# Attention with rope and a gated FFN: high parts of the rope rows on ScalarE, low parts first on GpSimd, swaps ahead of a transpose, span 0 held twice

## The reference

```python
q_pe = _rope(q_pe, cos, sin)            # the 64 rope rows of every query
k_pe = _rope(k_pe[:, None, :, :], cos, sin)
qs = concat([q_nope, q_pe]); ks_ = concat([k_nope, k_pe])
scores = einsum('bhqd,bhkd->bhqk', qs, ks_) * scale
scores = where(causal, scores, finfo.min)
attn = softmax(scores)
out = einsum('bhqk,bhkd->bhqd', attn, v) @ wo
```

## Time and profile before

| what | value |
|---|---|
| runs before | 1123.23 us median of 3 (1123.19 to 1127.71) |
| profiled execution | 1121.26 us, its span 1119.5 us |
| mean granted TensorE clock | 0.949 |
| busy share | PE 88%, PEld 75%, DVE 69%, ACT 67%, POOL 70% |

### The profile page before, as it was taken

The page is one execution under the profiler, slowest core; times in us unless marked ns, Lnnn a source line. Parts: engine busy times, 40 slices in busy tenths (PEclk is TensorE's granted clock), DMA queues, the critical chain, the costliest instruction groups (busy, mean ns, idle before and its releaser), DMA issues.

```text
span 1119.5 us, 26361 instructions
## 1 busy us (share of the span) xinstructions
PE 980.7 (88%) x10560; PEld 837.8 (75%) x10560; DVE 775.7 (69%) x1095; ACT 750.6 (67%) x1093; POOL 783.0 (70%) x576
## 2 busy tenths in 40 slices
PE   5558998989898989898989899988989896879998
PEld 5547777878687868786878777777878785768887
DVE  5747777877776778777787777867777787653134
ACT  1328687878686868777778777777778785752232
POOL 3656969596959796978688858877797877822331
PEclk7869999999998999999999989999999999889999
DMA  5019999999999999999989998899999999992001
GB/s 165 9 48 178 159 176 171 191 159 180 173 170 165 180 171 183 171 168 169 181 165 180 164 173 165 168 161 179 176 167 179 173 169 192 181 171 76 1 19 58
DMA packets 591979, 170.24 MB, mean 152 GB/s; under 512 B 574064, under 2 KB 585968, under 8 KB 591856
## 3 DMA queue, kind: packets, MB, share of 16 engines
q1 hardware_dynamic: 587376, 167.89, 83.1%
q10 hardware_dynamic: 4480, 0.66, 0.4%
HBM read 15.41 MB, written 2.10 MB: 16 GB/s over the span
## 4 chain that ended last, share of the span: by engine, by line
POOL 40%; PE 20%; DMA 9%; issue 8%; SPq 8%; ACT 7%; DVE 6%; ACTq 1%; POOLq 0%
POOL hl L1105 18%; PE s_ps L528 9%; POOL pe L1105 6%; PE s_ps L626 5%; DMA pT<-hl 5%; POOL QB_lo L1105 4%; POOL q_swap L1105 4%; DMA q_swap<-q_pe 3%; ACT hl L731 3%; SPq L471 3%; SPq L457 3%; POOL QA_lo L1105 3%; ACT prob L804 3%; POOL QA_hi L1105 3%; DVE hl L952 2%
## 5 line engine op out<-in xcount | busy, mean ns | idle before, releaser
L1105 POOL TENSOR_TENSOR hl<-prob,hl 128x1024 f16<-128x1024 f32 (+4 forms) x256 | 386.1, 1508 | 111.3 <-ACT hl L731 95.6
L804 ACT ACTIVATE prob<-s_ps,neg_max 128x1024 f32<-128x1024 f32 (+7 forms) x384 | 318.2, 863 | 184.8 <-POOL hl L1105 132.8
L943 DVE TENSOR_REDUCE part_max<-s_ps 128x1 f32<-128x1024 f32 (+7 forms) x256 | 245.4, 988 | 182.5 <-PE s_ps L626 165.8
L731 ACT ACTIVATE hl<-prob 128x1024 f16<-128x1024 f32 (+7 forms) x384 | 296.5, 806 | 25.3 <-DMA pT<-hl 23.4
L642 PE MATMUL o_ps<-v,pT 128*128 128x65 f16 x2176 | 232.3, 195 | 14.6 <-DMA pT<-hl 12.2
L643 PE MATMUL o_ps<-v,pT 128*128 128x64 f16 x2176 | 232.6, 197 | 0.0
L644 PE MATMUL o_ps<-v,pT 128*128 128x65 f16 x2176 | 231.3, 193 | 0.0
L952 DVE TENSOR_TENSOR hl<-prob,hl 128x1024 f16<-128x1024 f32 (+3 forms) x128 | 203.8, 1592 | 38.3 <-ACT hl L731 37.1
L642 PEld LDWEIGHTS o_ps<-v,pT 128*128 128x128 f16 x2176 | 206.5, 98 | 16.5 <-DMA pT<-hl 13.9
L644 PEld LDWEIGHTS o_ps<-v,pT 128*128 128x128 f16 x2176 | 205.8, 100 | 0.0
L643 PEld LDWEIGHTS o_ps<-v,pT 128*128 128x128 f16 x2176 | 205.2, 98 | 0.0
(11 more groups left out here) (183 smaller groups left out, 1992.1 us busy)
## 6 DMA issues: line engine op xcount, KB each, us to landing
q_swap<-q_pe SPq DMA_DIRECT2D x128, 64.0 KB, 2.0
pT<-hl SPq DMA_TRANSPOSE x256, 4.7
wq_sb<-in_L_attn_wq_dram SPq DMA_DIRECT2D x8, 384.0 KB, 4.1
acc<-in_L_attn_x_dram SPq DMA_DIRECT2D x4, 512.0 KB, 6.5
wo_sb<-in_L_attn_wo_dram SPq DMA_DIRECT2D x8, 256.0 KB, 3.2
x_in<-in_L_attn_x_dram SPq DMA_DIRECT2D x1, 2048.0 KB, 8.3
out_dram<-y SPq DMA_DIRECT2D x8, 256.0 KB, 2.1
wkvs<-in_L_attn_wkv_b_dram SPq DMA_DIRECT2D x8, 128.0 KB, 4.0
```

What stands on the lines that cost most here:

```text
L731: return nc.scalar.activation(dst, src, ACT.Copy)
L804: nc.scalar.activation(prob_of(u, m), score_bank(u, m), ACT.Exp, bias=neg_max[:, r:r + 1]).then_inc(exp_done, 1)
L943: nc.vector.tensor_reduce(part_max[:, u % 2, m:m + 1], src, AX.X, ALU.max).then_inc(part_done, 1)
L1105: return lambda: nc.gpsimd.tensor_tensor(dst, a, b, op)
```

## The change

- ScalarE's `rope_of_b` becomes `rope_high`: after `rope.2` it makes the high part of head A, the copy `pe_b`, and the high part of head B, three copies instead of one, and waits for the former group's `B..lo`. It stands in units 3, 5, 11 and 13 (before, the single copy stood in 4, 6, 12 and 14). GpSimd's eight high parts a pair fall away. `pe_b` is held once.
- GpSimd's order in a unit is `low`, `rest`, steps. A group has its three rope steps in one unit (2, 4, 10, 12) and both low parts in the next (3, 5, 11, 13). `wkvs`, `wpe_hi` and `wpe_lo` stay in their units.
- SP issues the swaps of a unit ahead of its `turn_first`.
- `prob0` is held twice; the exponential of span 0 of unit u waits for `low` of unit u-2.
- In the setup, the low parts of head B are made around `rope(0)`, and VectorE no longer makes the high part of head A.

```diff
-POOL_NEXT = {1: ["wkvs"], 6: ["wpe_hi"], 7: ["wpe_lo"], 10: rope(3)[:1], 11: rope(3)[1:] + ["A3hi"], 12: ["A3lo", rope(0)[0], "B3hi"],
...
+POOL_NEXT = {1: ["wkvs"], 6: ["wpe_hi"], 7: ["wpe_lo"], 10: rope(3), 11: ["A3lo", "B3lo"], 12: rope(0), 13: ["A0lo", "B0lo"]}
...
-        prob0 = ab("prob0", [P, W0])
+        prob0 = ab("prob0", [P, 2, W0])
...
             for u in range(NU):
                 pair, k = divmod(u, PU)
-                turn_first(u)
                 for name in jobs_at(u - 1):
                     if name[0].startswith("qB"):
                         swap(int(name[0][2:]), name[1])
+                turn_first(u)
                 turn_rest(u)
...
-            def rope_of_b(g, pair):
+            def rope_high(g, pair):
 
                 n = group_no(g, pair)
                 act.wait_ge(pool_done, POOL.after((f"rope{g}.2", pair)))
-                if n >= 2:
-                    before = GROUP_ORDER[(n - 2) % NG], (n - 2) // NG
+                if n >= 1:
+                    before = GROUP_ORDER[(n - 1) % NG], (n - 1) // NG
                     act.wait_ge(pool_done, POOL.after((f"B{before[0]}lo", before[1])))
-                copy(pe_b[:, n % 2, :], pe[ROPE:P, n % 2, :]).then_inc(rope_b, 1)
+                if pair > 0:
+                    act.wait_ge(scores_ready, queries_free(1, g, pair))
+                copy(queries(Q_hi, 0, g)[0:ROPE, :], pe[0:ROPE, n % 2, :])
+                copy(pe_b[:], pe[ROPE:P, n % 2, :])
+                copy(queries(Q_hi, 1, g)[0:ROPE, :], pe[ROPE:P, n % 2, :]).then_inc(rope_hi, 1)
 
             def exponentials(u, m):
                 act.wait_ge(max_ready, 2 * u + 1 + m // 2)
-                if m == 0 and u >= 1:
-                    act.wait_ge(pool_done, POOL.after(("low", u - 1)))
+                if m == 0 and u >= 2:
+                    act.wait_ge(pool_done, POOL.after(("low", u - 2)))
...
             for u in range(NU):
                 prob_low(u, 0)
+                prob_low(u, smaller(u))
                 for name in steps_at(u):
                     step(name)
-                prob_low(u, smaller(u))
```

More of the change, by code:

```diff
@@ L178, in rope @@
     return [f"rope{g}.{i}" for i in range(3)]
-def side(h, g):
-    return [f"{h}{g}hi", f"{h}{g}lo"]
 POOL_KEY = [[f"rms{n}"] + [f"kr{n}.{i}" for i in range(6)] for n in range(NG)]
@@ L188 @@
     f"rstd{n}" for n in range(NG)] + [(w, 0) for w in POOL_W] + POOL_KEY[0] + POOL_KEY[1] + [(r, 0) for r in rope(3)] + POOL_KEY[2] + POOL_KEY[3] + [
-    (r, 0) for r in rope(0)] + [(r, 0) for r in side("B", 3) + side("B", 0)]
-POOL_NEXT = {1: ["wkvs"], 6: ["wpe_hi"], 7: ["wpe_lo"], 10: rope(3)[:1], 11: rope(3)[1:] + ["A3hi"], 12: ["A3lo", rope(0)[0], "B3hi"],
-             13: ["B3lo"] + rope(0)[1:], 14: side("A", 0), 15: side("B", 0)}
-POOL_OWN = {2: rope(2)[:1], 3: rope(2)[1:] + ["A2hi"], 4: ["A2lo", rope(1)[0], "B2hi"], 5: ["B2lo"] + rope(1)[1:], 6: side("A", 1),
-            7: side("B", 1)}
+    (r, 0) for r in ["B3lo"] + rope(0) + ["B0lo"]]
+POOL_NEXT = {1: ["wkvs"], 6: ["wpe_hi"], 7: ["wpe_lo"], 10: rope(3), 11: ["A3lo", "B3lo"], 12: rope(0), 13: ["A0lo", "B0lo"]}
+POOL_OWN = {2: rope(2), 3: ["A2lo", "B2lo"], 4: rope(1), 5: ["A1lo", "B1lo"]}
 POOL_FFN = {6: ["up_zero", "up_scale_zero", "down_zero"], 8: ["up_scaled0", "up_scaled1"], 9: ["down_scaled"]}
-ROPE_B_OWN, ROPE_B_NEXT = {4: 2, 6: 1}, {12: 3, 14: 0}
+ROPE_HI_OWN, ROPE_HI_NEXT = {3: 2, 5: 1}, {11: 3, 13: 0}
 def steps_at(u):
@@ L207, in steps_at @@
     return steps
-POOL = Steps(POOL_SETUP + [name for u in range(NU) for name in [("low", u)] + steps_at(u) + [("rest", u)]])
+POOL = Steps(POOL_SETUP + [name for u in range(NU) for name in [("low", u), ("rest", u)] + steps_at(u)])
 def query_cols(g):
@@ L255, in mla_gated_ffn_kernel @@
         pe = ab("pe", [P, 2, BANK])
-        pe_b = ab("pe_b", [LORA, 2, BANK])
+        pe_b = ab("pe_b", [LORA, BANK])
         wq_sb = ab("wq_sb", [P, KE, QW])
@@ L361, in mla_gated_ffn_kernel @@
         queries_split = sem("queries_split")
-        swapped, rope_b = sem("swapped"), sem("rope_b")
+        swapped, rope_hi = sem("swapped"), sem("rope_hi")
         scores_ready, part_done, max_ready = sem("scores_ready"), sem("part_done"), sem("max_ready")
@@ L394, in prob_of @@
             w1 = width(u, 1)
-            return (prob0[:], prob12[:, u % 2, 0:w1], prob12[:, u % 2, w1:W12])[m]
+            return (prob0[:, u % 2, :], prob12[:, u % 2, 0:w1], prob12[:, u % 2, w1:W12])[m]
         def halves_of(u, m):
@@ L828, in _ @@
                 if name == ("qA0", 0):
-                    rope_of_b(3, 0)
-            rope_of_b(0, 0)
+                    rope_high(3, 0)
+            rope_high(0, 0)
             for u in range(NU + 1):
@@ L840, in _ @@
                     pair, k = divmod(u, PU)
[L841 to L844, removed]
+                    if k in ROPE_HI_OWN:
+                        rope_high(ROPE_HI_OWN[k], pair)
+                    if k in ROPE_HI_NEXT and pair < PAIRS - 1:
+                        rope_high(ROPE_HI_NEXT[k], pair + 1)
                     prob_high(u, 1)
@@ L1014, in split_first @@
                 hi, lo = queries(Q_hi, 0, g)[0:ROPE, :], queries(Q_lo, 0, g)[0:ROPE, :]
-                dve.wait_ge(pool_done, POOL.after((f"rope{g}.2", 0)))
-                then_wait(nc.vector.tensor_copy(hi, src))
+                dve.wait_ge(rope_hi, group_no(g, 0) + 1)
                 nc.vector.tensor_tensor(lo, src, f32(hi), ALU.subtract).then_inc(queries_split, 1)
@@ L1137, in split_step @@
                 n = group_no(g, pair)
-                src = (pe_b if head else pe)[0:ROPE, n % 2, :]
+                src = pe_b[:] if head else pe[0:ROPE, n % 2, :]
                 hi, lo = queries(Q_hi, head, g)[0:ROPE, :], queries(Q_lo, head, g)[0:ROPE, :]
[L1140 to L1145, removed]
+                run((name, pair), tt(lo, src, hi.bitcast(F32), ALU.subtract), (rope_hi, n + 1))
             def ffn_step(name):
                 if name == "up_zero":
-                    run(name, memset(up_raw[:, :, IT - 1, :], 0.0), (rope_b, NG * PAIRS))
+                    run(name, memset(up_raw[:, :, IT - 1, :], 0.0), (rope_hi, NG * PAIRS))
                 elif name == "up_scale_zero":
@@ L1228, in _ @@
             rotate_key(3)
+            split_step("B3lo", 0)
             for name in rope(0):
                 rope_step(name, 0)
-            for g in GROUP_ORDER[:2]:
-                for name in side("B", g):
-                    split_step(name, 0)
+            split_step("B0lo", 0)
             for u in range(NU):
                 prob_low(u, 0)
+                prob_low(u, smaller(u))
                 for name in steps_at(u):
                     step(name)
-                prob_low(u, smaller(u))
             for j in range(NG * IT):
```

## The result

| | median of runs | range | profiled execution | its span | mean granted clock |
|---|---|---|---|---|---|
| before | 1123.23 us (5 runs) | 1121.45 to 1127.71 | 1121.26 us | 1119.5 us | 0.949 |
| changed | 1112.44 us (5 runs) | 1110.08 to 1115.57 | 1112.44 us | 1110.6 us | 0.943 |

The ratio is 0.9917, with a 95% interval of 0.9893 to 0.994: faster by 0.8% by this ratio, and by 10.8 us (1.0%) on the two medians of the table. 1109 had been predicted.

A forecast was written before the change was run, and what follows sets the result against it. TensorE and GpSimd were taken to bound units by turns, some 17 us a pair lost to waits. 7.5 pairs at 2.1 us, less 1.4, gave 14.4 us: 1109 us, own range 1097 to 1117, 8 in 10 1080 to 1137.

The forecast's parts named there:

- The added wait: ScalarE waiting for `rope.2` before its copies: 3.7, 2.3, 2.2 and 3.0 us a pair, 60 to 110 us over the run.
- the slower rival: ScalarE's wait for `rope.2` dominates because the swap lands later: 1132 us, chance 0.23.
- The busy times: Expected engine totals: GpSimd busy near 705 us, ScalarE's copies 38 us more, GpSimd's swap wait still near 50 us.
- The second copy of span 0: ScalarE's exponential no longer waits for `low` of the unit before; unit 3 of pair 3 starts 1.4 us earlier.
- the first rival: The waits eat the whole gain, or the second copy doesn't help: 1117 to 1129, say 1122 us, chance 0.12.
- The gain per pair: Working over pair 3 gave 3.1 us won, less 0.8 for the clock leaves 2.3; 2.1 taken, for 7.5 pairs.
- one such stretch more in a pair: One more slow-clock stretch of TensorE behind unit 3's longer wait, half on the chain: 0.8 us a pair lost.
- the third rival: Every wait throttles TensorE, four slow stretches a pair instead of two: 1127 us; chance 0.07 no change, 0.05 slower.
- The start: In the setup, the first scores wait for three copies of 1.8 us instead of VectorE's 0.42: +1.4 us once.
- `turn_first` behind the swap: On SP, that transpose comes up to 3.0 us later in four units a pair, its product needed later: costed nothing.
- A sign: Listed as showing the forecast wrong: the pair's time changing in units 6 to 9, where no rope step stands.

## Why the prediction was right, and where its steps were not

**The added wait: right.** In pair 3 it was 3.33, 2.28, 3.01 and 2.59 us, where 3.7, 2.3, 2.2 and 3.0 stood in the working; 84.6 us in all, where 60 to 110 were expected. The sine step began 18.0 us after unit 1 (18.45 worked out), the copies ended so that unit 4 was 3.6 us late (4.1 worked out). In pair 3 SP's `turn_rest` of unit 1 took 2.73 us instead of 3.23, and the swap was not late, so the slower rival did not come.

**The busy times: right.** GpSimd 711 us (705), ScalarE +37 (38), the swap's wait 48 (50).

**The second copy of span 0, "1.4 us won": the step that failed.** Unit 3 did start 1.5 us earlier, but both runs that add or remove the copy (ratio 0.9982 on the kernel before, 1110.25 against 1112.44 us on the changed one) show no gain. The half of the first rival that "`hl` and `pT` stay two deep" is what happens on the kernel before, where `hl` waited 76.6 us. In the changed kernel it is another reason: the sum sets unit 4 (23.70 us after unit 1 without the copy, 23.76 with it), and its time doesn't hang on the start of unit 3.

**The gain per pair: mis-sized.** Over 7 pairs, from unit 1 of the first to unit 1 of the last, the changed kernel took 8.8 us less, 1.3 a pair instead of 2.1; the last pair and what follows took 4.0 less where about 1 was expected. In pair 3 the forecast held up to unit 9 (56.43 against 57.05 us from unit 1); then units 9 to 16 were to take 55.3 us and took 58.2, against 57.3 before. I had carried ScalarE's short units 12 and 14 on to the end of the pair; they came (5.9 and 4.5 us), but unit 15 then took 8.0 us instead of 6.6, with an exponential in it that waited 1.34 us for maxima. (The one behind it waited 1.63 us, as it had before.) That TensorE, held up in units 11 and 13, had its work still to do there is my reading and was not tested.

**That the total came so close is partly luck.** 14.4 us had been forecast; 10.8 came on the medians and 8.9 on the profiled executions, which can be taken apart. The seven pairs gave 5.9 us less than forecast and the rest of the kernel 2.9 more, and the start came 3.9 us later, where 1.4 had been worked out, for a reason that isn't the change's (below).

**The clock, "one such stretch more in a pair": not seen.** Windows by unit of pair 3: units 4 and 12, behind the two longer waits, and units 6 and 14, behind those of 2.28 and 2.59 us, against the earlier trace rows (the columns are those of the page: PE, PEld, DVE, ACT, POOL, then the granted clock):

```profile
453.28:459.94 6.66, 5.49 (x41) 4.54 (x42) 4.21 (x8) 6.25 (x10) 6.11 (x5) 0.74 1.14 162
...
468.52:473.54 5.02, 4.04 (x42) 3.35 (x40) 3.93 (x8) 5.02 (x11) 4.55 (x4) 1.00 1.04 193
...
510.20:516.05 5.85, 4.68 (x36) 4.17 (x37) 5.11 (x8) 5.76 (x9) 5.59 (x4) 0.71 1.12 181
...
524.94:529.48 4.54, 3.39 (x37) 3.02 (x38) 4.26 (x7) 4.45 (x7) 4.30 (x4) 1.00 1.02 190
```

At levels of 1.0 and 0.5, 0.74 over 6.66 us is 3.5 us at 1.2 GHz. Two such stretches stand in the pair, and two stood in the kernel before, in its units 7 and 14 by ScalarE's exponentials (the earlier trace rows is cut at GpSimd's `low`, where they fall in units 6 and 13). They only moved, behind the waits of 3.33 and 3.01 us, and the other fourteen units ran at 1.00. From unit 1 of pair 0 to unit 1 of pair 7 the mean granted clock was 0.97 before and 0.96 now. So the 0.8 us a pair that the forecast took off for the clock have no counterpart in pair 3; they happened to cover a part of the miss behind unit 9, which the working had left out. Two of four waits did not throttle the array, so the third rival did not come.

**The start, "+1.4": not seen.** The first exponential came at 81.64 us instead of 77.54, but ScalarE's first copy behind `rope.2` had started 4.4 us late already (72.21 against 67.79), and from there it took 9.4 us against 9.8. The delay is older than the change's first instruction, which starts at 54.31 us: ScalarE's copy `wc_hi`, at 36.74 us before, came at 40.98. The run without the second copy has the same setup code and its first exponential at 77.46. So the 4 us belong to that execution's setup, not to the change.

**`turn_first` behind the swap, costed at nothing: right in the changed kernel, for a reason that was only half looked at.** TensorE, the user that the working named, waited 5.7 us for `pT` (12.2 before), and 10.6 with the swap alone moved. But a second engine waits for the transpose: ScalarE may not overwrite `hl` before it is done. With the swap alone moved that wait doubled, from 23.4 us to 47.8. In the changed kernel it is 7.9, and 8.9 with the swap ahead and the order low, rest, steps on the kernel before.

**A sign that was badly chosen.** The pair's time was not to change in units 6 to 9. Units 6 to 8 took 17.4 us instead of 22.2, and the working itself had 3 x 5.6 = 16.8 for them, since the high parts leave them.

**What the prediction missed.** The parts don't add up to a small gain; they are large and of both signs. The moved swap alone gives 26 us; with the high parts on ScalarE as well and the steps spread, 38. The change as made is 30 us short of that. It puts cosine, sine and sum side by side, so the swap's flight has no step to lie under, `low` comes behind them and ScalarE's copies stand in the unit right after. I had followed these waits one by one, and priced them rightly, against the order before, but had not asked what each part would give in the other's absence. No run takes the 30 us apart cleanly, but two say where to look. The run with late copies and `pe_b` twice (ratio 1.0019) and the one with the steps spread (0.9647) have the same copies, buffers and swap; they differ by some 40 us, in the grouping, in `rest` ahead of the steps or behind, and in the units of the low parts. `rest` ahead of the steps gained time in both orders (7.6 us in the kernel before with the swap ahead, 58 in the changed one), so it isn't that. And within the grouped order the early copies are 13 us faster than the late ones. So the grouping costs, perhaps with the places of the low parts, and not the earlier copies.

## What to carry to other kernels

A step that waits for a DMA belongs behind other work of its engine that is due anyway, and the DMA's issue ahead of any transfer of its queue that nobody awaits soon; look at that first, since it is one moved line and was worth 26 us here, and 106 in the order with less cover. A buffer held twice took its own wait away here (132.8 us to 3.5) and handed it to the next buffer that is two deep and to the next engine: name that one before counting a gain. Where a transfer is moved back in a queue, count both the engine that reads its result and the one that may overwrite its source. When a change has several parts, run each alone on the kernel before; a small sum can hide a large gain.
